# First group's row maxima in a full-attention layer: score differences issued one block ahead, four result buffers, extra products on TensorE, fewer negated keys

## The reference, cut to what matters

```python
scores = jnp.einsum('bhqd,bhkd->bhqk', Q, K) * scale
attn = jax.nn.softmax(scores, axis=-1)
out = jnp.einsum('bhqk,bhkd->bhqd', attn, V)
out = out.transpose(0, 2, 1, 3).reshape(B, S, D)
return out @ Wo.T + bo
```

## Time and profile before

| what | value |
|---|---|
| median of three runs (lowest, highest) | 1149.72 us (1143.83, 1149.92) |
| profiled execution: span from first to last instruction | 1143.3 us |
| PE (TensorE matmul) busy | 1044.1 us, 91% |
| DVE (VectorE) busy | 925.3 us, 81% |
| ACT (ScalarE) busy | 709.0 us, 62% |
| POOL (GpSimd) busy | 461.7 us, 40% |
| mean granted TensorE clock over the span | 0.948 |

### The profile page before, as it was taken

The page is one execution under the profiler, slowest core; times in us unless marked ns, Lnnn a source line. Parts: engine busy times, 40 slices in busy tenths (PEclk is TensorE's granted clock), DMA queues, the critical chain, the costliest instruction groups (busy, mean ns, idle before and its releaser), DMA issues. The chain is left out here.

```text
span 1143.3 us, 18866 instructions
## 1 busy us (share of the span) xinstructions
PE 1044.1 (91%) x6314; PEld 427.5 (37%) x6314; DVE 925.3 (81%) x2139; ACT 709.0 (62%) x1089; POOL 461.7 (40%) x434
## 2 busy tenths in 40 slices
PE   5769999999999979999999998888888999999998
PEld 4212222222222325444444443334444444444443
DVE  8688999999998467889788776877876779877775
ACT  2537778777787765666666664355465566666664
POOL 4116336532100105565564554100113556556554
PEclk9758999999999989999999999679999999999999
DMA  6901302311200126566764873142206667687662
GB/s 207 253 2 28 81 9 72 80 53 28 54 2 1 43 59 170 163 170 174 196 181 140 218 193 81 34 110 59 72 4 172 157 152 188 171 208 193 182 189 57
DMA packets 72185, 131.63 MB, mean 115 GB/s; under 512 B 12680, under 2 KB 47624, under 8 KB 72088
## 3 DMA queue, kind: packets, MB, share of 16 engines
q1 hardware_dynamic: 68704, 120.92, 40.5%
q10 hardware_dynamic: 3384, 9.51, 3.1%
HBM read 115.08 MB, written 14.91 MB: 114 GB/s over the span
## 5 line engine op out<-in xcount | busy, mean ns | idle before, releaser
L421 ACT ACTIVATE Aatt_prob<-Aatt_st 128x1024 f32<-128x1024 f32 x256 | 247.7, 1022 | 66.1 <-PE Aatt_st L315 65.1
L487 DVE TENSOR_REDUCE Aatt_mx<-Aatt_sc 128x1 f32<-128x512 f32 x439 | 273.3, 683 | 10.0 <-PE Aatt_sc L302 9.5
L1993 POOL TENSOR_TENSOR M1ex_low<-M1ex_hid,M1ex_high 128x512 f16<-128x512 f32 x132 | 152.8, 1157 | 136.2 <-ACT M1ex_high L1892 70.1
L1993 POOL TENSOR_TENSOR M2ex_low<-M2ex_hid,M2ex_high 128x512 f16<-128x512 f32 x132 | 152.7, 1157 | 130.8 <-PE M2ex_acc L1848 73.3
L302 PE MATMUL Aatt_sc<-ks,qs 48*128 48x512 bf16 x496 | 152.5, 408 | 29.5 <-DVE Aatt_mx L487 11.8
L1886 ACT ACTIVATE M2ex_sil<-M2ex_ring,unscale 128x512 f32<-128x512 f32 x132 | 90.7, 687 | 95.3 <-PE M2ex_ring L1831 95.1
L1886 ACT ACTIVATE M1ex_sil<-M1ex_ring,unscale 128x512 f32<-128x512 f32 x132 | 90.7, 687 | 89.4 <-PE M1ex_ring L1831 88.9
L327 PE MATMUL Aatt_pv<-Aatt_prob,vg 128*32 128x512 f32 x1024 | 137.9, 611 | 0.6 <-ACT Aatt_prob L421 0.6
L1930 DVE SCALAR_TENSOR_TENSOR M2ex_ring<-M2ex_ring,unscale,M2ex_sil 128x512 f32<-128x512 f32 x132 | 100.0, 757 | 42.0 <-ACT M2ex_sil L1886 38.9
L1930 DVE SCALAR_TENSOR_TENSOR M1ex_ring<-M1ex_ring,unscale,M1ex_sil 128x512 f32<-128x512 f32 x132 | 99.9, 757 | 36.2 <-ACT M1ex_sil L1886 32.9
L302 PEld LDWEIGHTS Aatt_sc<-ks,qs 48*128 48x128 bf16 x496 | 35.9, 94 | 201.1 <-DVE Aatt_mx L487 167.7
(11 more groups left out here) (437 smaller groups left out, 1959.5 us busy)
## 6 DMA issues: line engine op xcount, KB each, us to landing
M1ex_cb<-comb SPq DMA_DIRECT2D x130, 256.0 KB, 4.1
M2ex_cb<-comb SPq DMA_DIRECT2D x130, 256.0 KB, 4.2
M_wt<-wsplit SPq DMA_DIRECT2D x132, 192.0 KB, 4.0
wsplit<-split_cut SPq DMA_DIRECT2D x9, 704.0 KB, 4.5
qs<-stack SPq DMA_DIRECT2D x32, 96.0 KB
ks<-stack SPq DMA_DIRECT2D x30, 96.0 KB
split_raw<-in_wg_dram ACTq DMA_DIRECT2D x3, 704.0 KB, 8.5
split_raw<-in_wu_dram ACTq DMA_DIRECT2D x3, 704.0 KB, 12.0
```

Source lines behind the costliest of these rows:

```text
L421: act.activation(prob[e % 4][:, :, :].rearrange("p a c -> p (a c)"), st[pr][:, :, :].rearrange("p a c -> p (a c)"), ACT.Exp, scale=SCALE). ...
L487: ins = dve.tensor_reduce(mx[k][:, m, h:h + 1], scores, AX.X, ALU.max)
L1993: pool.tensor_tensor(low[q % 3][:, :], hid[q % 3][:, :], high[q % 3][:, :], ALU.subtract).then_inc(low_ready, 1)
```

## The change

In group 0, TensorE issues the two differences of block b+1 ahead of the two rests of block b (in block 0, behind its four plain products). The step of the second batch's projections follows, as before, when all entries of the iteration are issued. The other engines keep their order. Differences and other products now count on two semaphores (`over_done` and `sc_done`). The Relu results have four buffers instead of two. From block 7 on two whole-array products of the identity with a key tile go into a bank that nobody reads (`warm`), and 36 more after the transposition of group 0's maxima. That transposition moves ahead of the fourth product of group 1's first block. GpSimd no longer negates the keys of groups 2 to 7. A tensor_scalar of the weight split gets a second operation, a multiplication by 1.0.

```diff
-        excess = [x[:, S:2 * S].bitcast(F32) for x in (env.xh, env.xl)]
+        excess = [x[:, c * S:(c + 1) * S].bitcast(F32) for c in range(2) for x in (env.xh, env.xl)]
+        IN_RING = len(excess)
...
-                pool.wait_ge(loaded[k], (n // 3) * LOADS + LOADS)
-                if n > 1:
-                    pool.wait_ge(sc_done, (n - 1) * NS)
+                pool.wait_ge(loaded[k], LOADS)
...
                 split_gpsimd(pool, weights, n)
-                if nxt2:
-                    negate(n + 2, (k + 2) % 3)
...
-                mm.then_inc(sc_done, 1)
+                mm.then_inc(over_done if kind == "excess" else sc_done, 1)
...
+            def warm(bank):
+
+                pe.matmul(bank, env.ident16[:, :], ks[0][:, 0, 0:CH], start=True, stop=True)
...
-            for n in range(2):
-                pe.wait_ge(loaded[n], LOADS)
-                for blk in range(STEPS if n == 0 else AHEAD):
-                    if n == 1 and 4 * blk == TURN_TILE:
-                        turn_max(0, 0, False)
-                    for part in range(4):
-                        score(n, n, blk, part)
-                    if n == 0:
-                        next(before, None)
+            pe.wait_ge(loaded[0], LOADS)
+            for blk in range(STEPS):
+                ahead = [(blk + 1, part) for part in range(2)] if blk + 1 < STEPS else []
+                now = [(blk, part) for part in (range(2, 4) if blk else range(4))]
+                for b, part in ahead + now if blk else now + ahead:
+                    score(0, 0, b, part)
+                next(before, None)
+                if blk >= SIDE_BLOCKS:
+                    for _ in range(WARM_BLOCK):
+                        warm(pv[:, :])
+            pe.wait_ge(loaded[1], LOADS)
             pe.wait_ge(v2.high_ready, 4)
             pe.wait_ge(v2.v_out, 2)
+            for blk in range(AHEAD):
+                for part in range(4):
+                    if (blk, part) == (0, 3):
+                        turn_max(0, 0, False)
+                        for _ in range(WARM_TOPS):
+                            warm(st[0][:, 0, :])
+                    score(1, 1, blk, part)
             pe.wait_ge(max_ready, MAX_IN)
             transposed(0, 0, 0, 0)
...
-                        act.wait_ge(sc_done, n * NS + 4 * blk + part + 1)
                         r = RANK[n, blk, part]
-                        if r > 2:
-                            act.wait_ge(red_done, RANK[USED[r - 3]])
+                        act.wait_ge(over_done, r)
+                        if r > IN_RING:
+                            act.wait_ge(red_done, RANK[USED[r - 1 - IN_RING]])
...
-        pool.tensor_scalar(raw, raw, w.scale[:, i:i + 1], None, ALU.mult).then_inc(w.scaled, 1)
+        pool.tensor_scalar(raw, raw, w.scale[:, i:i + 1], 1.0, ALU.mult, ALU.mult).then_inc(w.scaled, 1)
```

More of the change, by code:

```diff
@@ L94, in attend_full @@
     NS = 4 * STEPS
+    SIDE_BLOCKS, WARM_BLOCK, WARM_TOPS = 7, 2, 36
     with ExitStack() as ctx:
@@ L108, in attend_full @@
         pv = ps("pv", [P, CH], F32)
-        excess = [x[:, S:2 * S].bitcast(F32) for x in (env.xh, env.xl)]
+        excess = [x[:, c * S:(c + 1) * S].bitcast(F32) for c in range(2) for x in (env.xh, env.xl)]
+        IN_RING = len(excess)
         minus = [[env.wt[2 * a + jp][:, 0:4, :].rearrange("p a c -> p (a c)").bitcast(BF16) for jp in range(PAIR)] for a in range(2)]
         (v_ready, sc_done, red_done, m_step, turned, m_copied, max_ready,
-         st_done, exp_done, pv_done, u_out, excess_ready, minus_ready, mx_set) = map(sem, (
+         st_done, exp_done, pv_done, u_out, over_done, excess_ready, minus_ready, mx_set) = map(sem, (
             "v_ready", "sc_done", "red_done", "m_step", "turned", "m_copied",
-            "max_ready", "st_done", "exp_done", "pv_done", "u_out", "excess_ready", "minus_ready", "mx_set"))
+            "max_ready", "st_done", "exp_done", "pv_done", "u_out", "over_done", "excess_ready", "minus_ready", "mx_set"))
         weights = env.weights
@@ L179, in attend_full @@
                          if entries(n, blk)[part][0] != "excess") for n in range(NG)]
+        PLAIN = [sum(m < n and entries(m, b)[p][0] != "excess" for m, b, p in TURNS) for n in range(NG + 1)]
         USED = [turn for turn in TURNS if entries(*turn[:2])[turn[2]][0] == "rest"]
@@ L229, in _ @@
                 sp.wait_ge(weights.stored[i], 16 * len(range(i, len(PIECES), CUT_RING)))
-            sp.wait_ge(sc_done, NG * NS)
+            sp.wait_ge(sc_done, PLAIN[NG])
             for p in range(WT_RING):
@@ L410, in above @@
                     if entries(n, blk)[part][0] == "excess":
-                        act.wait_ge(sc_done, n * NS + 4 * blk + part + 1)
                         r = RANK[n, blk, part]
-                        if r > 2:
-                            act.wait_ge(red_done, RANK[USED[r - 3]])
-                        act.activation(excess[r % 2], sc_bank(n, 4 * blk + part), ACT.Relu).then_inc(excess_ready, 1)
+                        act.wait_ge(over_done, r)
+                        if r > IN_RING:
+                            act.wait_ge(red_done, RANK[USED[r - 1 - IN_RING]])
+                        act.activation(excess[r % IN_RING], sc_bank(n, 4 * blk + part), ACT.Relu).then_inc(excess_ready, 1)
             def exponential(n, s, pr):
@@ L484, in reduce_block @@
                     scores = sc_bank(n, 4 * blk + part)
-                    dve.wait_ge(sc_done, n * NS + 4 * blk + part + 1)
+                    dve.wait_ge(sc_done, RANK[n, blk, part])
                     if kind == "plain":
@@ L490, in reduce_block @@
                         dve.wait_ge(excess_ready, r)
-                        ins = dve.tensor_tensor_reduce(scores, scores, excess[r % 2], 1.0, LOWEST, ALU.add, ALU.max,
+                        ins = dve.tensor_tensor_reduce(scores, scores, excess[r % IN_RING], 1.0, LOWEST, ALU.add, ALU.max,
                                                        accum_out=mx[k][:, m, 0:1])
```

## The result

The changed kernel took 1166.82 us (median of four runs, 1163.34 to 1172.0) beside 1149.82 for the kernel before in the same comparison: a ratio of 1.0154, 95% interval 1.0111 to 1.0197. In a second comparison it took 1165.43 (four runs) beside 1151.24: 1.0143, 1.0088 to 1.0198. Slower, as forecast, by 14 to 17 us and not by 5.

The account below looks back on a forecast made before the run. VectorE's plain maxima bound 100 to 340 us, so their onset, near 96.5 us, moves the end. Terms 7.7 - 1.7 - 0.6 - 0.3 = +5.1 us on 1149.7 gave 1154.8 us; own range 1151 to 1158, wider range 1146 to 1166.

Parts of the forecast that it names:

- the ring: Group 0's projection blocks: projection, high, Relus, next differences, rests, projection again through ScalarE and TensorE; 4.14 us a block, 3.63 in block 1.
- rival A: The forecast itself: rings at full clock, net +1.6 to +8 us, around +5; chance 0.50.
- rival B: TensorE's clock falls to 0.50 in blocks 1 to 6, rings grow: 1160 us, or 1165 if blocks 7 to 15 stay slow; chance 0.25.
- Blocks 0 to 6, +7.7: Differences a block ahead make block 7's first sum later, 54.63 to 62.3 us; bounds +6.4 and +14.
- the bound of +14: Upper bound, in us, of the blocks 0 to 6 term, given for rival B.
- Blocks 7 to 15, -1.7: Late blocks of group 0 with two unread products each: 1.5 us a block, 15.2 becomes 13.5 us; bounds -3.1 and +3.6.
- The bound of +3.6 at 0.50: Upper bound for blocks 7 to 15: at clock 0.50 the pair of blocks takes 4.2 us.
- Four buffers, 0: They remove 1.7 us of waits around 51 to 55 us, but those blocks wait for the longer ring: 0, at most -1.7.
- Transposition and 36 products, 0: Earlier transposition gains nothing; the products, 7.9 us, lie beside VectorE's 9.24 us of weight maxima; 0 taken from 0 to 3.
- Group 1's blocks and the first steps, -0.9: Group 1's first blocks -0.6 us by shorter rests at the raised clock; the first steps' waits for score products -0.3.
- Negated keys and multiplication, 0: Nobody waits for GpSimd: 17.7 us less negating gains 0; the 3.84 us instruction could fall toward nothing or double, also 0.
- VectorE's pace, unchanged: From 100 to 340 us VectorE's plain maxima set the pace; the change leaves their count, so only their onset moves the end.

Follow-up runs that it names:

- products from block 0: Changed kernel with the two unread products in every block of group 0, not only from block 7 on; 1162.35 us, ratio 1.0096.
- one product a block: Version with differences ahead from block 7 and 128 unread products, one instead of two a block in blocks 7 to 15, 74 small ones instead of 65; 1153.12 us.

## Why the prediction was wrong

The sign and the place were right, and so were the ring and its steps; the clock at which the ring runs was not. The forecast took rival A where rival B's mechanism happened.

- **Blocks 0 to 6, +7.7: the step that failed.** It measured +14.5 (69.11 against 54.63). The start of the ring was right (second Relu of block 1 at 41.83, forecast 42.12). Three rings took 16.68 us (41.83 to 58.51) instead of 11.91: +4.8, because the steps on TensorE were priced at a clock of 1.00 and ran at 0.50. From there to block 7's first sum it took 10.60 instead of 8.3: +2.3. With products from block 0 this part still took 10.13, at a clock of 0.83 and with the products in TensorE's queue; how much of the 2.3 is the clock is not resolved. The prediction gave rival B 0.25 because the earlier trace rows have 0.97 with the projections in. That row is no evidence against B: it begins at 40.30, and from 36 to 40.3 us the kernel before was at 0.50 with a projection running (2.07 us for it, against 1.13 in the earlier trace rows). The clock had to rise in these very blocks, and the forecast took the rise for granted in a ring that has one projection product in 4.1 us where there had been one in 2.32. Rival B spoke of a fall; the clock never rose. B also missed the step from half to whole array (0.56 instead of 0.31), so a ring grew by 1.59, not 1.38. Its own terms give +13.0 here (7.7 + 5.3), not the bound of +14.
- **Blocks 7 to 15, -1.7.** Measured 13.99 us from block 7's first sum to T, 15.20 before: -1.2, at 1.58 to 1.60 us a block instead of 1.5. The clock brought it; at 0.50 the order alone has the old 1.72. The bound of +3.6 at 0.50 was real: one product a block at 0.50 made this part 17.5 us (54.00 to 71.47), +2.3.
- **Four buffers, 0.** True for the change as a whole, whose early blocks no longer wait on them, but for the wrong reason: with two, the lookahead is a ring of 3.26 us.
- **Transposition and 36 products, 0.** Right: 7.93 us beside weight maxima of 9.24. With one unread product a block, where they began at the low clock, they took 10.37.
- **Group 1's blocks and the first steps, -0.9.** Right in sum: +13.3 at T is +12.6 at the first exponential, +12.7 is +11.8 in the second profile. The clock fell behind the 36 products, as the prediction had weighed: 0.81 from 97 to 122.7, where the earlier trace rows have 1.00.
- **Negated keys and multiplication, 0.** Right for the time; the instruction fell from 3837 to 1439 ns, within the bounds that were given.
- **VectorE's pace, unchanged.** Right but for the row transfers: first to last exponential +0.3 and +2.4 us. The prediction had no term for what more instructions on TensorE do to the steps behind them.

The sum by these: 14.5 - 1.2 - 0.7 = 12.6 us at the first exponential, 12.9 at the last; in the second profiles the last is 13.3 later. The two comparisons have 17.0 and 14.2 us, with intervals (12.8 to 22.7 and 10.1 to 22.8) that hold both. What more the first may have is not resolved. The forecast had 5.1: of the 7.8 between it and the 12.9, 6.8 are the failed step and 0.5 the late blocks.

## What to carry to other kernels

Before an instruction with a wait is put ahead of others in a queue, close the ring: if what stands behind it feeds, through other engines, the thing that it waits for, the ring's length is the new pitch; here moving one product out from behind the wait undid 12.4 of 13.3 us. A new wait on TensorE is to be priced at both clock levels: ask where in the stage the clock rises today, and whether the new order still has what went before the rise. Unread products that don't bring the clock lengthened the pitch here (2.07 us instead of 1.72). Lookahead and buffers are one change.

## What the runs showed of the hardware

- GpSimd's tensor_scalar on 128x1408 float32 takes 3837 ns with one operation and 1439 ns with a second one that multiplies by 1.0. Start to start with the cast behind it, that is 3.90 us (132.82 to 136.72 before) and 1.51 (107.92 to 109.43 after).
- TensorE was busy 4.00 of 4.00 us at a granted 0.50 (58 to 62 us, one unread product a block), and 15.25 of 16.90 us at 1.00 with two (66 to 82.9 us of the changed kernel).
- With a packet of q8 (kind: instruction) 2.5 to 4.4 us ahead of it, the product that needs the 4 KB row transfers waited 0.63 to 1.28 us; without one, 0.18 to 0.20 (kernel before with and without 54 small products, both profiles of the changed kernel, changes of groups from 165 to 350 us). In the kernel before, 54 more products (108 instructions with their weight loads) near 20 us decided which.
- In the banded attention the same kernel had a clock of 0.90 in one execution and 0.75 in another, 130.0 and 142.4 us.
